# Row sums of a softmax: three matmul steps replaced by additions on VectorE and GpSimd

## What is computed

```python
def _L0_xattn_ref(x, cond, wq, bq, wkv, bkv, wp, bp):      # x: 8 x 512 x 512, cond: 8 x 1601 x 512
    H = 16                                                  # heads of 32 columns
    q = _qdq(x) @ _qdq(wq).T + bq
    kv = cond @ wkv.T + bkv
    ...
    attn = softmax(einsum('bnhd,bmhd->bhnm', q, k) * scale, axis=-1)
    o = einsum('bhnm,bmhd->bnhd', attn, v).reshape(B, N, C)
    return _qdq(o) @ _qdq(wp).T + bp
...
x = x + tanh(g_xattn) * _L0_xattn_ref(_layernorm(x), ctx_2048, ...)
x = x + tanh(g_ffn) * _L0_ffn_ref(_layernorm(x), ...)       # 32 experts, 4 of them per token, and a shared one
```

## Time and profile before

| | us |
|---|---|
| median of 3 runs | 3248.48 |
| lowest and highest | 3244.9, 3255.8 |
| the profiled execution | 3254.07 |
| its span, first to last instruction | 3251.4 |
| PE busy | 2811.8 (86%) |
| POOL busy | 1806.8 (56%) |
| DVE busy | 1727.0 (53%) |
| ACT busy | 1387.3 (43%) |

### The profile page before, as it was taken

One profiled execution on the slowest core, in us unless ns is written; L12 is line 12 of the kernel. 1 busy time (PEld: TensorE's weight loads), 2 busy tenths in 40 slices (PEclk: granted clock), 3 DMA queues, 4 the chain that ended last, 5 costly groups with the idle time before them and its releaser, 6 DMA issues. The chain is left out here.

```text
span 3251.4 us, 42577 instructions
## 1 busy us (share of the span) xinstructions
PE 2811.8 (86%) x14876; PEld 1192.9 (37%) x14876; DVE 1727.0 (53%) x2854; ACT 1387.3 (43%) x2460; POOL 1806.8 (56%) x1570
## 2 busy tenths in 40 slices
PE   5898988899889888988899898889888689996986
PEld 3223333333333333333333333333332344443765
DVE  6566556656565656566556655665653324342222
ACT  3155445644564455455545544564456211010111
POOL 0285566556655665657566656755669223324555
PEclk9799999899999999999999999999999789998999
DMA  4111012110211031103112101211011221222997
GB/s 127 33 44 52 21 34 70 52 35 20 78 48 44 11 97 39 34 21 92 29 34 69 52 21 34 69 52 34 21 51 29 79 89 66 78 78 73 271 279 194
DMA packets 146578, 215.53 MB, mean 66 GB/s; under 512 B 24984, under 2 KB 78232, under 8 KB 146368
## 3 DMA queue, kind: packets, MB, share of 16 engines
q1 hardware_dynamic: 130496, 195.95, 20.0%
q0 software_dynamic: 15872, 16.87, 2.8%
HBM read 126.49 MB, written 34.24 MB: 49 GB/s over the span
## 5 line engine op out<-in xcount | busy, mean ns | idle before, releaser
L1510 POOL TENSOR_TENSOR prob_acc<-prob_acc,probs 128x512 f32<-128x512 f32 x1152 | 1430.1, 1275 | 484.7 <-ACT probs L1038 484.2
L1038 ACT ACTIVATE probs<-s_ps 128x512 f32<-128x512 f32 (+1 forms) x1664 | 939.0, 596 | 806.8 <-PE s_ps L810 787.3
L1253 DVE TENSOR_REDUCE piece_max<-r_all 128x2 f32<-128x802 f32 (+1 forms) x1024 | 965.2, 986 | 229.1 <-PE r_all L732 223.6
L810 PE MATMUL s_ps<-q_stack,k_flat 97*128 97x512 f16 (+1 forms) x1664 | 630.0, 397 | 73.9 <-ACT probs L1038 66.0
L732 PE MATMUL r_all<-k_flat,q_stack 96*128 96x401 f16 (+1 forms) x2048 | 552.3, 353 | 131.7 <-DVE piece_max L1253 80.2
L824 PE MATMUL o_ps<-probs,v_sb 128*32 128x512 f32 (+1 forms) x3328 | 462.8, 629 | 21.4 <-ACT probs L1038 21.4
L810 PEld LDWEIGHTS s_ps<-q_stack,k_flat 97*128 97x128 f16 (+1 forms) x1664 | 161.5, 102 | 635.6 <-ACT probs L1038 411.5
L1507 POOL COPY prob_acc<-probs 128x512 f32<-128x512 f32 x128 | 72.8, 612 | 507.2 <-PE sum_ps L844 372.2
L732 PEld LDWEIGHTS r_all<-k_flat,q_stack 96*128 96x128 f16 x2048 | 178.3, 100 | 392.7 <-DVE piece_max L1253 143.1
L1542 POOL DMA_INDIRECT slot_rows<-payload,slot x128 | 125.3, 979 | 317.7 <-DVE slot L1440 194.7
L1246 DVE SCALAR_TENSOR_TENSOR k_lo<-r_all,bk_col,k_hi 128x400 f16<-128x400 f32 (+1 forms) x128 | 81.8, 639 | 280.7 <-ACT k_hi L996 280.7
(11 more groups left out here) (193 smaller groups left out, 2752.8 us busy)
## 6 DMA issues: line engine op xcount, KB each, us to landing
k_flat<-k_hi SPq DMA_DIRECT2D x256, 100.1 KB, 2.2
ctx_raw<-in_ctx SPq DMA_DIRECT2D x96, 256.0 KB, 2.9
v_sb<-in_L_ffn_w SPq DMA_DIRECT2D x48, 512.0 KB
xin<-in_x SPq DMA_DIRECT2D x16, 1024.0 KB, 5.6
k_flat<-k_lo SPq DMA_DIRECT2D x128, 100.1 KB, 2.2
ctx_hi<-in_L_ffn_w SPq DMA_DIRECT2D x24, 512.0 KB
ctx_lo<-in_L_ffn_w SPq DMA_DIRECT2D x24, 512.0 KB
q_stack<-q_hi SPq DMA_DIRECT2D x256, 32.0 KB, 1.8
```

The source lines that it names most:

```text
L810: nc.tensor.matmul(s_ps[j % SBANKS][0:w, :], k_stack[:, g % 2, j, kt * P:kt * P + w], q_stack[:, g % 2, j, :], start=True, stop=True).then ...
L1038: nc.scalar.activation(probs[0:w, slot, j, :], s_ps[j % SBANKS][0:w, :], ACT.Exp).then_inc(probs_ready, 1)
L1253: V.reduce_max(piece_max[:, j * TT + qt, 2 * i:2 * i + 2], r_all[:, k:k + 2, 0:MAX_WIDE[i]], X_AXIS).then_inc(free_of(*key), 1)
L1510: last = G.tensor_tensor(prob_acc[:, j, :], prob_acc[:, j, :], probs[:, slot, j, :], ALU.add)
```

## The change

Tiles 4, 8 and 12 leave PE. `sums_of` is gone, and `accumulated_sums` alone writes `sum_ps`.

- `merge(s, j)` on DVE, for tiles 3 and 7 (`MERGED`): in step 5 (and 9) DVE adds the probabilities of tile 3 (7) into those of tile 4 (8) in place, four additions of 128 x 512, two behind the third part of the fill and two behind the fourth. It waits for `heads_of` of tile 4 (8), which reads the tile unchanged.
- GpSimd adds tiles 1, 2, 4, 5, 6, 8, 9, 10 and 11 (`ADD_STEPS`). The first addition takes tiles 0 and 1, in place of the copy. That of tile 4 (8) waits for each head's merge. It adds the bias rows (`add_bias`, L1517) in step 7 in place of step 4.
- `add_last(n)` on DVE: in step 0 of the next group, behind the lead tiles, four additions of tile 12 (65 rows) into `prob_acc`, each behind GpSimd's addition of tile 11 for that head. `accumulated_sums` now waits for these (`last_added`).
- `exp_of` waits, before it overwrites a slot, for the merge, the GpSimd addition or the last addition that read it.

```diff
-POOL_STEPS = [kt for kt in range(KT) if kt not in (4, 8, KT - 1)]
-FIRST_SUMS = 4
+MERGED = (3, 7)
+ADD_STEPS = [kt for kt in range(1, KT - 1) if kt not in MERGED]
+BIAS_STEP = 7
...
             def accumulated_sums(n):
 
-                pe.wait_ge(probs_added, (n + 1) * len(POOL_STEPS) * GH)
+                if n:
+                    pe.wait_ge(sums_copied, n)
+                pe.wait_ge(last_added, (n + 1) * GH)
                 for j in range(GH):
                     last = nc.tensor.matmul(sum_ps[j * DH:(j + 1) * DH, :], ones[:, :], prob_acc[:, j, :],
-                                            start=False, stop=True)
+                                            start=True, stop=True)
...
-                if kt and (kt - 1) not in POOL_STEPS:
-                    sums_of(s - 1)
...
-                if before >= 0 and before % KT in POOL_STEPS:
-                    act.wait_ge(probs_added, adds_before(before) * GH + j + 1)
+                if before >= 0 and before % KT == KT - 1:
+                    act.wait_ge(last_added, before // KT * GH + j + 1)
+                elif before >= 0 and before % KT in MERGED:
+                    act.wait_ge(probs_merged, merge_of(before) * GH + j + 1)
+                elif before >= 0:
+                    act.wait_ge(probs_added, add_of(before) * GH + j + 1)
...
+            def merge(s, j):
+
+                if j == 0:
+                    dve.wait_ge(probs_used, s + 1)
+                dve.wait_ge(probs_ready, s * GH + j + 1)
+                into = probs[:, s % HALVES, j, :]
+                V.tensor_tensor(into, into, probs[:, (s - 1) % HALVES, j, :], ALU.add).then_inc(probs_merged, 1)
+
+            def add_last(n):
+
+                s = n * KT + KT - 1
+                w = rows(KT - 1)
+                for j in range(GH):
+                    dve.wait_ge(probs_ready, s * GH + j + 1)
+                    dve.wait_ge(probs_added, ((n + 1) * len(ADD_STEPS) - 1) * GH + j + 1)
+                    V.tensor_tensor(prob_acc[0:w, j, :], prob_acc[0:w, j, :], probs[0:w, s % HALVES, j, :], ALU.add
+                                    ).then_inc(last_added, 1)
...
-                for key in lead_tiles(b, g, kt) + fill_tiles(b, g, kt):
+                s = step_of(b, g, kt)
+                for key in lead_tiles(b, g, kt):
                     tile(key)
+                if kt == 0 and s:
+                    add_last(s // KT - 1)
+                fill = fill_tiles(b, g, kt)
+                for j in range(GH):
+                    for key in fill[len(fill) * j // GH:len(fill) * (j + 1) // GH]:
+                        tile(key)
+                    if kt - 2 in MERGED and j >= SBANKS:
+                        merge(s - 1, 2 * (j - SBANKS))
+                        merge(s - 1, 2 * (j - SBANKS) + 1)
...
                 for j in range(GH):
-                    pool.wait_ge(probs_ready, s * GH + j + 1)
+                    if s % KT - 1 in MERGED:
+                        pool.wait_ge(probs_merged, merge_of(s - 1) * GH + j + 1)
+                    else:
+                        pool.wait_ge(probs_ready, s * GH + j + 1)
                     if first:
-                        step.carry_wait()
-                        last = G.tensor_copy(prob_acc[:, j, :], probs[:, slot, j, :])
+                        other = probs[:, (s - 1) % HALVES, j, :]
                     else:
                         pool.wait_ge(probs_added, (n - 1) * GH + j + 1)
-                        last = G.tensor_tensor(prob_acc[:, j, :], prob_acc[:, j, :], probs[:, slot, j, :], ALU.add)
-                    last.then_inc(probs_added, 1)
+                        other = prob_acc[:, j, :]
+                    G.tensor_tensor(prob_acc[:, j, :], other, probs[:, slot, j, :], ALU.add).then_inc(probs_added, 1)
```

More of the change, by code:

```diff
@@ L76, in step_of, with add_of, merge_of @@
     return group(b, g) * KT + kt
-def adds_before(s):
-    return (s // KT) * len(POOL_STEPS) + POOL_STEPS.index(s % KT)
+def add_of(s):
+    return (s // KT) * len(ADD_STEPS) + ADD_STEPS.index(max(s % KT, 1))
+def merge_of(s):
+    return (s // KT) * len(MERGED) + MERGED.index(s % KT)
 def key_tiles(b, g):
@@ L431, in build @@
         probs_added = sem("probs_added")
+        probs_merged = sem("probs_merged")
+        last_added = sem("last_added")
         acc_summed = sem("acc_summed")
@@ L825, in heads_of @@
                                             probs[0:w, slot, j, :], start=(kt == 0), stop=(kt == KT - 1))
-                if kt in POOL_STEPS:
-                    last.then_inc(probs_used, 1)
-            def sums_of(s):
-                kt = s % KT
-                w, slot = rows(kt), s % HALVES
-                if kt == FIRST_SUMS and s >= KT:
-                    pe.wait_ge(sums_copied, s // KT)
-                for j in range(GH):
-                    last = nc.tensor.matmul(sum_ps[j * DH:(j + 1) * DH, :], ones[0:w, :], probs[0:w, slot, j, :],
-                                            start=(kt == FIRST_SUMS), stop=False)
                 last.then_inc(probs_used, 1)
             def accumulated_sums(n):
-                pe.wait_ge(probs_added, (n + 1) * len(POOL_STEPS) * GH)
+                if n:
+                    pe.wait_ge(sums_copied, n)
+                pe.wait_ge(last_added, (n + 1) * GH)
                 for j in range(GH):
                     last = nc.tensor.matmul(sum_ps[j * DH:(j + 1) * DH, :], ones[:, :], prob_acc[:, j, :],
-                                            start=False, stop=True)
+                                            start=True, stop=True)
                 last.then_inc(acc_summed, 1)
@@ L869, in _ @@
             heads_of(last_step)
-            sums_of(last_step)
             accumulated_sums(B * GROUPS - 1)
@@ L1301, in _ @@
                     h_part(b - 1, kt)
+            add_last(B * GROUPS - 1)
             heads_out(B - 1, GROUPS - 1)
@@ L1497, in add_probs @@
             def add_probs(s):
-                slot, n = s % HALVES, adds_before(s)
-                first = s % KT == POOL_STEPS[0]
+                slot, n = s % HALVES, add_of(s)
+                first = s % KT == ADD_STEPS[0]
                 if first and s >= KT:
@@ L1522, in _ @@
             for b, g, kt in steps():
-                if kt in POOL_STEPS:
+                if kt in ADD_STEPS:
                     add_probs(step_of(b, g, kt))
-                elif g == 0 and kt == FIRST_SUMS and b:
+                elif g == 0 and kt == BIAS_STEP and b:
                     add_bias(b - 1)
```

1 line of the change is left out of this document (removed).

## The result

| | before | after |
|---|---|---|
| median, us | 3246.69 (4 runs) | 3607.05 (4 runs) |
| lowest and highest | 3239.12, 3255.8 | 3591.95, 3609.56 |
| span of the profiled execution | 3251.4 | 3606.9 |

The ratio is 1.110 (1.107 to 1.114): 360 us slower, where 206 were forecast. The direction was right, and the time lies above the range.

A forecast was written before the change was run, and what follows sets the result against it. The prediction took DVE's place in a step, and the PSUM banks it keeps from PE, as the bound. Groups' terms of 67, 54, 47, 35 and 7 us gave +210, so about 3453 us, range 3325 to 3485.

The forecast's parts named there:

- What bounds the kernel: Whole kernel: what matters is where in a step DVE gets new work and how long it keeps PSUM banks from PE.
- The price of a merge: Merge on DVE: 0.61 us, or 0.61 + 1.1 us where a POOL addition is under way.
- The first rival: No exclusion between merge and POOL addition, merge always 0.61 us: 92 us, 3345; chance 0.24, shared with half the effect.
- The sum: All groups together: +210 us on the profiled 3254.07, less 5, so 3459; median about 3453 us.
- Group's end: Step 0 of the next group: four last additions take 2.5 us, PE waits; net +0.85 us, 31 times.
- Bursts: Merges in steps 5 and 9 delay the maxima PE needs: +1.2 to +4.7 us each, 177 us in all.
- Step 9: Group 1's second burst: +3.2 us from DVE; POOL's chain ends about when exp wants its slot, nothing added.
- The last group: No maxima; POOL sets the end, waiting for the merge in step 5, then 28 additions: +6.7 us.
- PE busy some 100 us less: Sign in the profile after: L836 gone and PE's busy time some 100 us less.
- POOL is the bound: Rival: 12 POOL additions per group behind merges each stand another 0.46 us; 77 us, 3530; chance 0.06.
- No exclusion: Rival: a merge never waits for a POOL addition; 92 us, 3345; chance 0.24, shared with half the effect.
- Faster: Rival: PE's own stream decides, DVE's additions fit its idle time; 3205 us, or 3145 with group's end hidden; chance 0.06.

The follow-up runs named there:

- e11_burst_alone: Kernel before, with four unread maxima of 512 columns on DVE at the places of the merges: 3353.12 us, ratio 1.030.
- e2_last_only: Kernel before, with tile 12 alone moved to `add_last` on DVE; tiles 4 and 8 stay on PE: 3333.0 us, ratio 1.026.
- e1_last_on_pe: Changed kernel, with tile 12 summed by PE again and the merges kept on DVE: 3529.58 us, ratio 1.087.
- e6_last_only_busy: Kernel before with tile 12 alone on DVE, plus eight unread matmuls in PE's wait ahead of the accumulated sums: 3285.96 us, ratio 1.013.
- e3_merge_reads_psum: Changed kernel, with merges that take the minimum of a PSUM tile and the neighbour instead of adding two SBUF tiles: 3479.43 us, ratio 1.072.
- e5_busy_waits: Changed kernel, with eight unread matmuls per merge burst on PE around the third max tile of steps 6 and 10: 3581.72 us, ratio 1.105.
- e7_last_early: Kernel before with tile 12 alone on DVE, its last additions placed ahead of the lead tiles: 3219.75 us, ratio 0.992.
- e9_all_four_and_early: Changed kernel, with GpSimd's first addition behind a burst waiting for all four merges, and last additions ahead of the lead tiles: 3418.29 us, ratio 1.051.
- e10_merges_spread: Changed kernel with GpSimd waiting for all four merges, last additions early, and merges spread singly over steps 5 and 6 (9 and 10): 3531.31 us, ratio 1.086.

## Why the prediction was wrong, point by point

**What bounds the kernel: right.** DVE's place in the step and the banks it keeps from PE decide, and shares of busy time mislead. `e11_burst_alone` shows it with DVE work that does nothing else.

**The price of a merge: right.** Forecast 0.61 to 0.69 for the first and about 1.7 for the fourth; 0.68 and 1.75 were measured, and the burst took 4.6 us for 4.7. The exclusion, read from one clip and one POOL maximum, holds for a two-input addition as well (up to 1762 ns), and its worth was near too: 118 forecast, 104 and 128 measured. That nearness is partly luck, since the 118 are all at full clock and the measured gains hold 154 and 184 us less of half clock. The Trainium skill's rule (SBUF — State Buffer, Who interferes with whom) agrees with the bursts. It has the second one wait for the first to end, and the last section shows waits of several additions; there the measurement decides. (The first rival's terms add to 92, not the 95 named beside the rule, and give 3340, not 3345.)

**The sum: too small, in each term but two.** The step that failed is the one that turns a delay into a price. It took each delay as it reaches PE and priced what follows at the durations of before, all read at 2.4 GHz. In truth PE often goes on at 1.2 GHz after it has stood. The forecast of 210 us with 103 us of work gone meant that PE would stand for 313 us more; it stood for 251 more, and slower matmuls made up 209. How much of those 209 lies beside a DVE that is late anyway is shown for the groups' ends alone.
- *Group's end*, 0.85 forecast 31 times, 26 us: 87 by `e2_last_only`, 77 by `e1_last_on_pe`, 76 by the steps. 47 of it are the clock; with the clock held, the steps cost 28 (`e6_last_only_busy`). The wait of 1.8 us was right.
- *Bursts*, 177 us forecast: 261 by the steps. Without exclusion the prediction priced them at 60 (its 92 less the ends and the last group); DVE's time alone costs 97 (`e11_burst_alone`, which keeps the sums of tiles 4 and 8 on PE, 68 us of work), and what is left besides exclusion and the groups' ends is about 3479 - 87 - 3247 = 145 us (`e3_merge_reads_psum`). The 97 us come with 104 us more half clock; how much of them it causes isn't shown, but at most 50 of them are slower matmuls. `e5_busy_waits` gives back 25 us net in the changed kernel. So for the bursts the clock is a part of what was missing, and its size stays open.
- *Step 9*, where "I add nothing" stood for POOL's chain: that was nearly right. Exp waits for GpSimd 42 us in all and for the merges 24, against 11.7 us before, but in step 9 itself it waits for GpSimd only 4.5 us in the whole kernel, against 1.1. What the term missed behind step 9 (155 us for 89) is there in large part with DVE's time alone (75 us, with 80 us more half clock). In `e3_merge_reads_psum` the two waits of exp are 21 and 23 us; they may be a part of the 48 us between 97 and 145, which stay open otherwise.
- *The last group*, 7 forecast: 18. The steps cost 10 of it. The other 8 are a single last addition on DVE, below.

**"PE busy some 100 us less": wrong**, 110 more, by the same step. PE's waits for the maxima grew to 238 us, less than the "several hundred". A group g = 1 grew by 11.9 us (6 to 7 forecast), g = 3 by 9.1 (5).

**The rivals.** "POOL is the bound" came nearest in size (3530) with a cause that the runs don't bear out: making GpSimd wait longer made the kernel faster by 104 us. "No exclusion" fell with the merges' 1762 ns. "Faster" asked for idle time of 2.5 us in a step and the next; `e7_last_early` shows what was left of it: 25 us (0.8%) of the 33 (31 x 1.07) that tile 12's sums took, with the additions moved to where nobody waits for them. That PE's clock would turn was no rival at all, though before's slices have an 8 and 7s in them.

## What to carry to other kernels

Price a new wait of the bounding matrix engine twice: once as the time it stands, once as a stretch behind it that may run at half clock (28 of the first 30 group ends in `e2_last_only`, 22 of 30 in the changed kernel); and look in the profile for slices at a lower clock before taking matmul durations from one at full clock. Moving work from a busy TensorE to an idle engine paid here only where TensorE didn't take that engine's next product at once; where the work went in that engine's stream mattered more than what it costs (3333 against 3220 us for the same four additions). Between VectorE and GpSimd, try to let one finish its run before the other starts, by a wait if need be: 104 us for one changed constant.

## What the runs showed of the hardware

**A wait can be worth filling.** In `e2_last_only` a wait of 1.71 us was followed by 3.4 us at 1.2 GHz, in the burst above PE's waits (the last of 1.37 us) by 6.8. Eight matmuls that nobody reads, put into it, made `e6_last_only_busy` 47 us faster than `e2_last_only`.

**DVE's addition can stand through a whole run of GpSimd.** In a burst the two engines alternate, and one stands for one addition of the other at most (1762 ns the longest merge, 1742 the longest POOL addition). At a group's end that isn't always so. The last additions in the changed kernel (ns), and those before the last sums:

```profile
L1302 DVE TENSOR_TENSOR prob_acc<-prob_acc,probs x128: 676/680/8981, 208.7 to 2888.1; 65x512 f32<-65x512 f32 x128
...
2877.97 10.79 DVE L1302 TENSOR_TENSOR prob_acc<-prob_acc,probs 65x512 f32<-65x512 f32 x4 [14.70 <-POOL prob_acc L1540]
```

The first of these four began at 2877.97, 0.16 us after GpSimd had begun an addition, and ended at 2886.95, 8981 ns later: only after that addition, two more, and the four bias additions behind them, which GpSimd issued without a pause up to 2886.40. PE waited 12.4 us for it. In `e9_all_four_and_early` and `e10_merges_spread` 24 and 23 of the last additions took 4.10 to 4.13 us, each until the end of three additions of GpSimd, of which the first had begun some 0.15 us earlier.

What decides this stays open. It is neither the 65 rows nor the tile that both write, alone: in `e10_merges_spread` the first of the four last additions begins, in each of the 32 groups, 0.13 to 0.16 us behind the start of a GpSimd addition, and 8 of them, with these same rows and this tile, stood for one addition only. GpSimd had no pause there either; its next additions stood for DVE in turn. One of these places:

```profile
622.16 5.61 DVE L1302 TENSOR_TENSOR prob_acc<-prob_acc,probs 65x512 f32<-65x512 f32 x4 [4.87 <-POOL prob_acc L1541]
617.13 9.50 POOL L1541 TENSOR_TENSOR prob_acc<-prob_acc,probs 128x512 f32<-128x512 f32 x7
```

The first of the four takes 1667 ns here, as a merge in a burst does.
